# A graph layer on one core: the third part of a message written as bf16 into the upper halves of its words

## The reference

```
mask = jnp.clip(jax.nn.sigmoid(log_alpha) * (ZETA - GAMMA) + GAMMA, 0.0, 1.0)
rowsum = jax.ops.segment_sum(mask, row, num_segments=n) + 1e-06
d_inv_sqrt = jnp.clip(rowsum ** (-0.5), 0.0, 10.0)
vals = mask * d_inv_sqrt[row] * d_inv_sqrt[col]
x = jax.ops.segment_sum(vals[:, None] * x[col], row, num_segments=n)
out = out + x
```

## Time and profile before

| what | value |
|---|---|
| median of 3 runs | 4210.95 us (4206.87 to 4211.45) |
| the profiled execution's own time | 4212.77 us |
| its span in the trace | 4211.1 us |
| TensorE busy | 3738.5 us (89% of the span) |
| VectorE busy | 3609.0 us (86%) |
| GpSimd busy | 2393.5 us (57%) |
| ScalarE busy | 2012.5 us (48%) |
| the three message stages | 439 + 440 + 440 us, about 1319 us of the span |

### The profile page before, as it was taken

The page is one execution under the profiler, slowest core; times in us unless marked ns, Lnnn a source line. Parts: engine busy times, 40 slices in busy tenths (PEclk is TensorE's granted clock), DMA queues, the critical chain, the costliest instruction groups (busy, mean ns, idle before and its releaser), DMA issues. The chain is left out here.

```text
span 4211.1 us, 258179 instructions
## 1 busy us (share of the span) xinstructions
PE 3738.5 (89%) x99727; PEld 3559.3 (85%) x99728; DVE 3609.0 (86%) x5865; ACT 2012.5 (48%) x5107; POOL 2393.5 (57%) x3286
## 2 busy tenths in 40 slices
PE   5888678888679999799988999799997999979998
PEld 4777568888669999799978999799995999979997
DVE  7999968888758888899977888799995888879998
ACT  4889768888621111466641111256662111136664
POOL 3776433333233333699972333299994333349998
PEclk8888789999889999899989999999998999989999
DMA  1000089999637777466636777566662677756665
GB/s 36 15 14 15 14 280 336 342 332 343 239 115 247 251 251 247 139 180 180 181 85 206 247 250 252 168 192 180 180 180 80 234 248 251 251 155 181 180 180 144
DMA packets 586262, 800.02 MB, mean 190 GB/s; under 512 B 126790, under 2 KB 528154, under 8 KB 586170
## 3 DMA queue, kind: packets, MB, share of 16 engines
q1 hardware_dynamic: 550106, 719.89, 54.6%
q0 software_dynamic: 36064, 78.85, 6.3%
HBM read 672.34 MB, written 126.04 MB: 190 GB/s over the span
## 5 line engine op out<-in xcount | busy, mean ns | idle before, releaser
L1246 PE MATMUL pre_ps<-rows_a,hotT_a 128*128 128x64 bf16 x21609 | 1300.6, 193 | 54.3 <-DMA hotT_a<-hot_scratch 27.4
L1551 POOL TENSOR_TENSOR message<-message 128x448 f32<-128x448 f32 x1029 | 1306.5, 1306 | 66.3 <-ACT message L1535 66.2
L1246 PE MATMUL pre_ps<-table,hotT_a 128*128 128x64 bf16 x21609 | 1299.8, 193 | 2.4 <-issue 2.4
L1246 PEld LDWEIGHTS pre_ps<-rows_a,hotT_a 128*128 128x128 fp8e4 x21609 | 1129.0, 98 | 80.4 <-issue 63.6
L1246 PEld LDWEIGHTS pre_ps<-table,hotT_a 128*128 128x128 fp8e4 x21609 | 1131.9, 98 | 1.7 <-issue 1.7
L1562 DVE TENSOR_TENSOR message<-message 128x448 f32<-128x448 f32 x1029 | 1004.6, 977 | 0.0
L1535 ACT ACTIVATE message<-high_ps,mask 128x64 f32<-128x64 f32 x3087 | 742.8, 311 | 465.0 <-PE high_ps L1494 442.5
L1362 DVE SCALAR_TENSOR_TENSOR weighed<-pre_ps,w 128x448 f32<-128x448 f32 x1029 | 642.5, 624 | 277.8 <-PE pre_ps L1246 190.5
L1506 PE MATMUL sum_ps<-message,hot_b 128*128 128x192 bf16 x7203 | 783.3, 247 | 4.7 <-DVE message L1562 4.6
L1348 DVE TENSOR_REDUCE logit<-weighed 128x7 f32<-128x448 f32 x1029 | 626.0, 609 | 0.0
L1494 PE MATMUL low_ps<-table,hot_b 128*128 128x64 bf16 x12348 | 529.9, 193 | 101.7 <-DMA hot_b<-hot_scratch 56.5
(11 more groups left out here) (160 smaller groups left out, 5117.3 us busy)
## 6 DMA issues: line engine op xcount, KB each, us to landing
hotT_a<-hot_scratch SPq DMA_DIRECT2D x1029, 224.0 KB, 4.4
hot_b<-hot_scratch SPq DMA_DIRECT2D x1029, 224.0 KB, 2.8
hot_scratch<-hot SPq DMA_DIRECT2D x343, 336.0 KB, 6.0
hot_a<-hot_scratch SPq DMA_DIRECT2D x147, 784.0 KB, 5.1
places<-slots_scratch POOLq DMA_DIRECT2D x196, 224.0 KB, 6.5
places<-slots_scratch POOLq DMA_DIRECT2D x98, 336.0 KB, 7.3
slots_scratch<-bins SPq DMA_DIRECT2D x392, 16.0 KB, 1.4
out<-res SPq DMA_DIRECT2D x1, 1536.0 KB
```

What stands on the lines that cost most here:

```text
L1246: last = nc.tensor.matmul(pre_ps[g][:, j, :], hotT[:, b, g, end, j * P:(j + 1) * P].bitcast(FP8), table, start=end + part == 0, stop=end = ...
L1551: pool.tensor_tensor(message[:, g, :, 1, :], message[:, g, :, 0, :], top[:, g, :, 0, :, 1], ALU.subtract).then_inc(s["rest_ready"], 1)
```

## The change

`third` keeps its two inputs, its operation, its place in the order, its wait and its signal. Its output is another view of the same words: in place of 4-byte float32 values in part 2, it writes 2-byte bf16 values into the upper halves of the words of part 2. In a row of 64 features the values lie 4 bytes apart as before; the lower halves are no longer written, and nobody reads them. The value that TensorE reads is now rounded to bf16, where before it was cut off. No other instruction changes, on any engine.

```
                 def third(q, r, g, b):
                     dve.wait_ge(s["rest_ready"], q + 1)
-                    dve.tensor_tensor(message[:, g, :, 2, :], message[:, g, :, 1, :], top[:, g, :, 1, :, 1],
+                    dve.tensor_tensor(top[:, g, :, 2, :, 1], message[:, g, :, 1, :], top[:, g, :, 1, :, 1],
                                       ALU.subtract).then_inc(s["third_ready"], 1)
```

## The result

The changed kernel takes 4221.48 us in the median of 11 runs (4213.32 to 4226.29), the kernel before 4210.95 (4204.65 to 4214.77), also 11. The ratio is 1.0025, with a 95% interval of 1.0017 to 1.0032: slower by 0.25%, some 10 us, just over the 0.2% that I set for "no change". The profiled execution has a span of 4216.9 us.

What follows compares the result with a forecast made beforehand. VectorE and GpSimd, taking turns, were held to bound the message stages, with TensorE close behind. Four terms of 0 added to the profiled 4212.8 us; as a median the forecast was 4211, range 4200 to 4226.

Steps and rivals of the forecast that it cites:

- Term 3: Output spacing of `third`: gaps between 2-byte values cost 0, taken between bounds of 0 and 394 ns a `third`.
- What bounds the stage: Message stages, 31% of the span: held by VectorE and GpSimd, not TensorE, which has 0.063 us a group to spare.
- Term 1: Inputs of `third`: unchanged, cost nothing; reading 2-byte values 4 bytes apart costs 1 ns at most.
- term 2: Output width of `third`: bf16 alone makes it neither quicker nor slower; -1 us in all, taken as 0.
- Term 4: VectorE's share of the turn: GpSimd is kept out just as long, L1551 and TensorE's gaps stay; 0.
- no change because the price is hidden: `third` gets longer outside its turn, up to 376 ns of cover; period stays, time 4211; chance about 0.03.
- my sign for it: Profile of `third` under a hidden price: still 1015 ns, only its uncontended minimum rising above 610.
- The slower rival's small version: Write of `third`: a fixed 10 to 15 ns at the instruction's end, giving 4221 to 4226; chance about 0.04.
- Its larger versions: Write of `third`: gaps cost up to 394 ns, giving 4618, or 4230 if GpSimd enters early; all slower versions 0.12.
- the faster rival: VectorE's turn is released sooner as half the bytes land sooner; 4191 to 4201 likelier, 4146 at most; chance 0.07.
- My reading of turns: VectorE and GpSimd take turns on something both need: about 0.37 and 0.9 us, making the 1.27 us period.
- my price for a third turn: VectorE's extra instruction in the message stage: a fixed cost per turn, 100 ns or more, would eat the gain.

Runs made afterwards that it cites:

- bench_forms: Kernel before plus a bench behind its last stage timing the subtraction of `third` in several output forms; at 448 elements upper halves cost 32 ns more, packed bf16 nothing.
- own_psum: Kernel before with one of GpSimd's seven buckets given to VectorE, which takes the value again from PSUM; 4657.21 us, ratio 1.1060.
- the split kernels: Kernel before with one or two of GpSimd's seven buckets subtracted by VectorE in an extra instruction; 4469.38 us (ratio 1.0623) and 4589.52 us (1.0905).
- the bench: Kernel before plus the message stage's VectorE and GpSimd pattern beside other engines' work; with TensorE, 28 groups took 35.16 us (upper halves) against 34.92 (float32).
- bench_stage: Kernel before plus a bench with more output steps, and VectorE and GpSimd in the stage's pattern, other engines at rest; 1272.0 and 1272.4 ns a group.
- bench_tensor: Kernel before plus a bench varying TensorE's matmuls, with and without GpSimd's subtraction; without it, upper halves 876.4 ns a pair with TensorE at work, 866.7 at rest.

## Why the prediction was right or wrong

The time lay in the range (4200 to 4226), and the forecast of no change was off by 0.25%, just over the 0.2% that I had set for it. That it came so near was in part luck. Term 3 at 0 was wrong, and 33 ns a `third`, had they been paid, would be 1029 x 33 = 34 us and 4245, outside the range. They were hidden, and I had given that a chance of 0.03.

- **What bounds the stage** was right: VectorE and GpSimd in turns, TensorE with idle time to spare before and after.
- **Term 1** (inputs, 0) and **term 2** (bf16 as such, 0) were right: packed bf16 gave 625 against 625 ns alone and 611/1015 in the stage.
- **Term 3** (spacing of the output) is the step that failed, in its size: I took 0 between bounds of 0 and 394 ns. It measured 32 ns a `third` alone and 34 in the stage (610 to 644), 0.07 ns an element. The argument for 0 was that float32 writes and half-word reads at 4 bytes were both free; neither is a half-word write. The row that I set aside, GpSimd's at 6 bytes, had the kind right. VectorE at 6 bytes paid 282 ns, 0.63 an element against GpSimd's 0.88, while GpSimd at 4 bytes paid 3 ns (935 against 932 alone in bench_forms). The Trainium skill's access granule (Vector Engine (DVE) Microarchitecture Reference, "Measured stream behaviour on trn2") would have given an estimate of 296 ns if half words counted as hops; the measurement of 32 decides against that reading. By the same rule float32 in every other word should be slow, and the trace does not agree: it took 625 ns, as packed, and only every fourth word took 950.
- **Term 4** (the turn stays as long, nothing late) was right for the two engines alone: 35.28 against 35.27 us for 28 groups. It was wrong with TensorE at work: 9 ns a group go through. I had named TensorE only as a bound, never as a neighbour that makes a write dearer. The introduction says that the engines meet only at semaphores. The turns and this price show that VectorE and GpSimd also hold each other up, and that TensorE's work slows VectorE, where no semaphore stands.
- **The rival "no change because the price is hidden"** was the right mechanism for the 33 ns, and my sign for it was nearly so: the minimum rose above 610, but the median rose as well (by 43 ns), since what overlaps the next instruction is counted in it. **The slower rival's small version**, 10 to 15 ns, at 0.04, came nearest to the time, with 8 to 9 ns a group; its "fixed time at the end" was not the cause, since the price is per element. Its larger versions and the faster rival found nothing.
- **My reading of turns** fits own_psum and the split kernels, in which `third` waits for whole subtractions; my price for a third turn there did not. The waiting is the exclusive turn of the Trainium skill (SBUF — State Buffer, "Who interferes with whom"), and the trace of own_psum agrees: 1.15 us against 0.61.

What stays open: why a half-filled word costs VectorE time at all, and how TensorE's work makes its write dearer. It is shown that TensorE's activity does it, with reads of any tile and without GpSimd, and that reading at gaps does more than reading packed. What weight loads, short matmuls and the writes to PSUM add was not separated, nor why that part isn't hidden where the 33 ns are. The effect of TensorE was shown in the bench, not by taking it away in the stage, where it can't be.

## What to carry to other kernels

Price a 2-byte output by how it fills words, not by its type. In this subtraction of 448 elements it cost, packed, what float32 costs; in every other half 5% more; in every fourth half 84% more, where float32 in every other word was free. An instruction that seems hidden in another engine's turn should be measured with all neighbours at work, since the 0 of two engines became 9 ns a group with a third. And where two engines alternate by whole instructions, the place of an instruction in the order of issue can be worth more than its length: moving a seventh or two of the work to the faster engine cost 6 to 11% here.

## What was not expected of the hardware

- VectorE alone, 448 elements, two SBUF inputs (bench_forms, bench_stage): bf16 output at 2, 4, 6, 8 and 16 bytes took 625, 656, 907, 1153 and 2141 ns; float32 at 4, 8 and 16 bytes 625, 625 and 950.
- GpSimd alone, same subtraction (bench_forms): float32 932 ns, packed 932, upper halves 935.
- TensorE's work took VectorE's pair of L1577 and `third` from 866.7 to 876.4 ns with half words; float32 beside the same work had 866.7 (bench_tensor, GpSimd at rest).
